# Layer 0 of a CIN tower: from one fp32 product to three fp32r products per sum

## The reference

```python
e = jnp.stack([tbl_f[ids[:, f]] for f in range(39)], axis=1)      # [1024, 39, 16]
x0 = xk = e
for W in (f0, f1, f2):                  # [39*39, 128], [128*39, 128], [128*39, 128]
    z = einsum('bfd,bgd->bfgd', x0, xk).reshape(b, f * g, d)
    xk = einsum('bpd,pm->bmd', z, W)    # [b, 128, 16]
    outs.append(xk)
z = concatenate(outs, axis=1).sum(-1)   # [1024, 384]
h = concatenate([z, dense_ctx], axis=1) # [1024, 400]
h = relu(h @ W_top1 + b_top1); h = relu(h @ W_top2 + b_top2)
y = h @ W_top3                          # [1024, 1]
```

## Time and profile before

| | us |
|---|---|
| median of 3 runs | 1385.07 |
| profiled execution | 1389.53 |
| its span, first to last instruction | 1387.5 |
| TensorE busy | 1304.8 |
| VectorE busy | 1125.3 |
| ScalarE busy | 907.9 |
| GpSimd busy | 703.4 |

### The profile page before, as it was taken

How to read it: one execution, slowest core, us unless ns; L and a number is a source line. 1 busy time by engine, 2 the same in 40 slices (tenths; PEclk the granted TensorE clock), 3 DMA queues, 4 the chain that set the end, 5 groups by cost and what they waited for, 6 DMA issues and landing times.

```text
span 1387.5 us, 20075 instructions
## 1 busy us (share of the span) xinstructions
PE 1304.8 (94%) x5856; PEld 987.6 (71%) x5856; DVE 1125.3 (81%) x2794; ACT 907.9 (65%) x3233; POOL 703.4 (51%) x697
## 2 busy tenths in 40 slices
PE   1189999999999999999999999999999999999998
PEld 0156776777777777777777777777777777777787
DVE  0178988888888888888888888888888888888875
ACT  1046776766767676677767667676766777676664
POOL 6687556654545556454566545455564532333200
PEclk9999999999999999999999999999999999999999
DMA  4081021100311012110211003110121102110000
GB/s 104 17 236 44 21 70 50 49 27 4 94 31 43 27 35 70 50 30 13 70 50 49 28 3 94 31 42 27 35 71 49 30 12 68 47 47 27 1 1 1
DMA packets 52266, 62.47 MB, mean 45 GB/s; under 512 B 13619, under 2 KB 25637, under 8 KB 52156
## 3 DMA queue, kind: packets, MB, share of 16 engines
q1 hardware_dynamic: 34554, 54.64, 12.8%
q0 software_dynamic: 10128, 2.98, 2.1%
q10 hardware_dynamic: 7473, 3.56, 1.0%
HBM read 10.02 MB, written 0.00 MB: 7 GB/s over the span
## 4 chain that ended last, share of the span: by engine, by line
PE 88%; DVE 4%; ACT 3%; issue 3%; ACTq 2%; DMA 1%; SPq 0%; DVEq 0%
PE Y L749 20%; PE Y L751 19%; PE Y L750 19%; PE C L697 14%; PE C L711 5%; PE S L705 5%; ACT Y L473 2%; ACTq L237 2%; PE C L729 1%; PE S L671 1%; DMA G<-in_L_rec_f_dram 1%; DVE sum_b L616 1%; DVE sum_a L616 1%; PE C L719 1%; ACT h L480 1%
## 5 line engine op out<-in xcount | busy, mean ns | idle before, releaser
L473 ACT ACTIVATE Y<-Y,x_col 128x128 f32<-128x128 f32 x2944 | 801.4, 358 | 391.8 <-PE Y L751 351.0
L749 PE MATMUL Y<-f_high,cur_high 128*128 128x512 f32 (+1 forms) x1280 | 627.0, 490 | 8.7 <-DVE part L629 3.5
L751 PE MATMUL Y<-f_high,cur_low 128*128 128x512 f32 (+1 forms) x1280 | 497.6, 389 | 0.0
L750 PE MATMUL Y<-f_low,cur_high 128*128 128x512 f32 (+1 forms) x1280 | 496.9, 388 | 0.0
L373 POOL TENSOR_TENSOR pairs<-shifted,base 117x512 f32<-117x512 f32 x186 | 240.6, 1295 | 462.8 <-PE C L697 460.9
L335 POOL DMA_INDIRECT rows<-in_tbl_dram,ids_sb x312 | 304.9, 977 | 82.4 <-issue 64.9
L749 PEld LDWEIGHTS Y<-f_high,cur_high 128*128 128x128 f32 x1280 | 240.6, 188 | 121.4 <-issue 47.5
L750 PEld LDWEIGHTS Y<-f_low,cur_high 128*128 128x128 f32 x1280 | 241.6, 189 | 92.0 <-issue 52.2
L751 PEld LDWEIGHTS Y<-f_high,cur_low 128*128 128x128 f32 x1280 | 240.0, 188 | 50.8
L616 DVE SCALAR_TENSOR_TENSOR sum_b<-Y,x_col,sum_b 128x128 f32<-128x128 f32 x768 | 262.1, 341 | 0.0
L697 PE MATMUL C<-pairs,f_sum 117*128 117x512 f32 (+1 forms) x448 | 230.0, 596 | 6.4 <-DVE pairs L579 6.2
(11 more groups left out here) (80 smaller groups left out, 643.6 us busy)
## 6 DMA issues: line engine op xcount, KB each, us to landing
shifted<-x_seq SPq DMA_DIRECT2D x157, 234.0 KB
base<-x_seq SPq DMA_DIRECT2D x95, 78.0 KB
rows<-in_tbl_dram,ids_sb POOLq DMA_INDIRECT x312
shifted<-x_seq SPq DMA_DIRECT2D x31, 156.0 KB
G<-in_L_rec_f_dram ACTq DMA_DIRECT2D x3, 832.0 KB, 6.0
w_sb<-in_W_top_dram SPq DMA_DIRECT2D x1, 768.0 KB
w_sb<-in_W_top_dram SPq DMA_DIRECT2D x1, 512.0 KB
shifted<-x_seq ACTq DMA_DIRECT2D x2, 234.0 KB
```

The costliest lines, as they stand in the source:

```text
L473: ins = act.activation(where[:, i * M:(i + 1) * M], where[:, i * M:(i + 1) * M], ACT.Copy, scale=x_col[:, t // JT % QG, t % JT, f:f + 1])
L749: pe.matmul(where, ch, wh, start=True, stop=False)
L750: pe.matmul(where, ch, wl, start=False, stop=False)
L751: pe.matmul(where, cl, wh, start=False, stop=True).then_inc(y_filled, 1)
```

## The change

Layer 0's sum becomes three fp32r products: high weights with high products, low weights with high products, high weights with low products.

- ScalarE rounds each piece of products to fp32r (`round_pair`, a Copy of up to 117x512 from SBUF to SBUF) at given slots of its program, behind that slot's scaling.
- GpSimd subtracts the rounded from the exact piece (`pair_low`). In group 0 VectorE does it (`first_pair_low`).
- The exact products have a ring of two buffers, high and low parts rings of three. So `pair` waits for the low part of two pieces before, `round_pair` for the sum of three pieces before, and the sum for its low part.
- The weights are split once at the start: VectorE adds the mirrored halves into `f0_direct`, ScalarE rounds them, VectorE subtracts.
- The sums move to slots 9, 12, 15, 18, 21, 25, 28; in groups with an MLP they stay at 12 to 30. The roundings stand behind slots 38 (piece 0, a group ahead), 1, 5, 10, 14, 18, 20; in groups with an MLP behind 4, 8, 14, 15, 19, 21. For a group with q = 0 (and group 1) piece 0 isn't rounded ahead: its pieces 0, 1, 2 are rounded behind slots 1, 4, 8.
- GpSimd makes the products 0 and 1 a group ahead, at tile 3. Its steps for tiles 0 to 2 hold four operations each, with a gather behind each as far as there are any.
- 18 gathers of batch tile 1 instead of 16 are made before group 0, three of them behind the first spreading; later gathers are shared 2, 2, 2, 3 over the four tiles of a group.
- `sum_a`, `sum_b` and `part` lose their second buffer; `h1`, `h2`, `y` and `y_col` lie in `rows_seq`. ScalarE issues the output's DMAs, one for each batch tile, instead of SP's two.

```diff
 RING = 3
+PAIR_RING = 2
-AT_SUM = [12 + 3 * k for k in range(K0)]
+AT_SUM = [9, 12, 15, 18, 21, 25, 28]
+AT_SUM_MLP = [12, 15, 18, 21, 24, 27, 30]
+AT_ROUND = [None, 1, 5, 10, 14, 18, 20]
+AT_ROUND_MLP = [1, 4, 8, 14, 15, 19, 21]
+ROUND_AHEAD = 38
-EARLY = 16
-FIRST_EARLY = 4
+EARLY = 18
+FIRST_EARLY, LAST_EARLY = 4, 3
+GATHER_SHARE = (2, 2, 2, 3)
+def first_round_ahead(g):
+    return g % QG != 0 and g >= 2
+def rounds_in_group(g):
+    places = AT_ROUND_MLP if mlp_in_group(g) is not None else AT_ROUND
+    if first_round_ahead(g + 1):
+        return [None] + places[1:]
+    return AT_ROUND_MLP[:3] + places[3:]
...
             def pair(g, k):
-                pool.wait_ge(cur0_summed, z - RING + 1)
...
+                if g == 1 and k < PAIR_RING:
+                    pool.wait_ge(first_low, K0)
+                else:
+                    pool.wait_ge(low_ready, z - K0 - PAIR_RING + 1)
+            def pair_low(g, k):
+                pool.wait_ge(pairs_rounded, z + 1)
+                pool.tensor_tensor(pairs_low[0:r, z % RING, :], pairs[0:r, z % PAIR_RING, :],
+                                   pairs_high[0:r, z % RING, :].bitcast(F32), ALU.subtract).then_inc(low_ready, 1)
+            LOW_STEPS = ((("low", 0), ("pair", 2), ("low", 1), ("pair", 3)),
+                         (("low", 2), ("pair", 4), ("low", 3), ("pair", 5)),
+                         (("low", 4), ("pair", 6), ("low", 5), ("low", 6)),
+                         ())
...
-            gather(1, range(FIRST_EARLY, EARLY))
+            gather(1, range(FIRST_EARLY, EARLY - LAST_EARLY))
+            for k in (0, 1):
+                pair(1, k)
...
             spread(0)
+            gather(1, range(EARLY - LAST_EARLY, EARLY))
...
+                    if j == JT - 1 and g + 2 < NG and first_round_ahead(g + 2):
+                        for k in (0, 1):
+                            pair(g + 2, k)
...
                     if j == JT - 1 and g + 1 < NG:
                         spread(g + 1)
+                    if j == JT - 1 and g + 2 < NG and not first_round_ahead(g + 2):
+                        for k in (0, 1):
+                            pair(g + 2, k)
...
+            def round_pair(g, k):
+                if g:
+                    act.wait_ge(pairs_ready, z - K0 + 1)
+                else:
+                    act.wait_ge(first_pairs, k + 1)
+                if z >= RING:
+                    act.wait_ge(cur0_summed, z - RING + 1)
+                act.activation(pairs_high[0:r, z % RING, :], pairs[0:r, z % PAIR_RING, :], ACT.Copy)\
+                   .then_inc(pairs_rounded, 1)
...
+            def first_pair_low(k):
+                dve.wait_ge(pairs_rounded, k + 1)
+                dve.tensor_tensor(pairs_low[0:r, k % RING, :], pairs[0:r, k % PAIR_RING, :],
+                                  pairs_high[0:r, k % RING, :].bitcast(F32), ALU.subtract).then_inc(first_low, 1)
...
-                    pe.wait_ge(pairs_ready, z - K0 + 1)
+                    pe.wait_ge(low_ready, z - K0 + 1)
...
-                pe.matmul(C[:], f0_sum[0:r, k, :], pairs[0:r, z % RING, :],
-                          start=k == 0, stop=k == K0 - 1).then_inc(cur0_summed, 1)
+                high, low = pairs_high[0:r, z % RING, :], pairs_low[0:r, z % RING, :]
+                pe.matmul(C[:], f0_sum[0:r, k, :], high, start=k == 0, stop=False)
+                pe.matmul(C[:], f0_low[0:r, k, :], high, start=False, stop=False)
+                pe.matmul(C[:], f0_sum[0:r, k, :], low, start=False, stop=k == K0 - 1).then_inc(cur0_summed, 1)
```

More of the change, by code:

```diff
@@ L126, in gathers_in_tile @@
     step, u = divmod(t + AHEAD, TPB)
-    u, tiles = u - 2, TPB - 2
-    if step + 1 >= BT or u < 0:
-        return None
-    return step + 1, range(NF * u // tiles, NF * (u + 1) // tiles)
+    if step + 1 >= BT or u < 2:
+        return None
+    share = [GATHER_SHARE[(v - AHEAD) % JT] for v in range(2, TPB)]
+    done, all_ = sum(share[:u - 2]), sum(share)
+    return step + 1, range(NF * done // all_, NF * (done + share[u - 2]) // all_)
 def build(nc, dense, ids, tables, w1, b1, w2, b2, w3, f0, f1, f2, out):
@@ L312, in _ @@
                                  allow_slow_non_contiguous=True).then_inc(mlp_in, 16)
[L313 to L318, removed]
+            sp.wait_ge(y_out, 16 * BT)
         @blk.gpsimd
@@ L396, in _ @@
                         pool.wait_ge(rows_taken, len(ROW_PARTS) * (now[0] - 1))
-                    if q == 1 and j >= 2 and bt + 1 < BT:
-                        for part in ((0, 1), (2, 3))[j - 2]:
-                            take_rows(bt + 1, part)
[L400 to L403, removed]
+                    if j == JT - 1 and g + 2 < NG and first_round_ahead(g + 2):
+                        for k in (0, 1):
+                            pair(g + 2, k)
+                    if q == 1 and j == JT - 1 and bt + 1 < BT:
+                        for part in (2, 3):
+                            take_rows(bt + 1, part)
+                    steps = LOW_STEPS[j] if g + 1 < NG else ()
+                    for i in range(max(len(steps), len(fs))):
+                        if i < len(steps):
+                            kind, k = steps[i]
+                            (pair if kind == "pair" else pair_low)(g + 1, k)
                         if i < len(fs):
@@ L407, in _ @@
                         spread(g + 1)
+                    if j == JT - 1 and g + 2 < NG and not first_round_ahead(g + 2):
+                        for k in (0, 1):
+                            pair(g + 2, k)
+                    if q == 1 and j == JT - 2 and bt + 1 < BT:
+                        for part in (0, 1):
+                            take_rows(bt + 1, part)
         @blk.scalar
@@ L602, in fuse @@
                 for i, f in enumerate(CH_F[c]):
-                    acc = (sum_a if c < 4 else part, sum_b)[(i + starts) % 2][:, t % 2, :]
+                    acc = (sum_a[:] if c < 4 else part[:], sum_b[:])[(i + starts) % 2]
                     src = bank(t, c)[:, i * M:(i + 1) * M]
```

101 lines of the change are left out of this document (72 added, 29 removed).

## The result

The changed kernel takes 1397.39 us (median of 4 runs, 1395.9 to 1398.19) against 1385.17; the ratio is 1.0083, 95% interval 1.0071 to 1.0095. Forecast was 1377.5, range 1361 to 1395. The profiled execution took 1396.6 us, its span is 1394.9, granted clock 0.996. Against the earlier trace rows, its page: engines, chain, sums.

What follows compares the result with a forecast made beforehand. The prediction took TensorE, 94% busy, to bound the kernel, with little slack in the ring with ScalarE and VectorE. A start cost of 11.1 us less 18.6 us gained in groups gave -7.5 us, so 1377.5 us, range 1361 to 1395.

Steps and rivals of the forecast that it cites:

- The price of one sum: On TensorE, one layer 0 sum falls from 0.86 to 0.70 us as three fp32r products 0.23 us apart.
- The start: Before the first chunk, VectorE's added subtractions and waits for roundings put the first chunk at 86.8 us, +3.4.
- Group 0: First group: GpSimd's queue has the low part of product 6 at 120.7 us, TensorE wants it at about 113.
- q = 0: Groups with the MLP, 41.8 us: sums keep their places, 1.1 less 0.2 for a GpSimd wait, gain 0.9.
- q = 1: Steady group, 39.5 us: ScalarE's block of 15 scalings, lengthened by two roundings, then VectorE; 38.9, gain 0.6.
- They push slot 18 back by 0.6: 39.5, gain 1.0: Groups with q = 2, 40.5 us: sixteen transposes delay slot 18 by 0.6, giving 39.5 us.
- I get 40.4, a loss of 0.2: Groups with q = 3, 40.2 us: late GpSimd products, product 6 ready at 23.5 us, hold ScalarE's rounding and scalings.
- Groups 1 to 4: Groups without layer 2, where TensorE waits for VectorE: some 1.2 us gained in three, nothing in the fourth, 3.7.
- The sum: Whole kernel: +11.1 us at the start and -18.6 in the groups make -7.5 us, median 1377.5.
- Rival 2: GpSimd and in-order ScalarE form a loop at slot 20's rounding, 0.3 to 0.8 us per group: +2 to +16; chance 0.27.
- Rival 1: TensorE bounds everywhere: -34 + 11 = -23 us, 1362 us; chance 0.15.
- The rule weighed: GpSimd and two-SBUF-input VectorE instructions lock a shared port: steady state untouched, start 10 us more by the slow row.

Runs made afterwards that it cites:

- e1: Changed kernel without the gathers for batch tiles 1 to 7, which use the rows of the first: 1376.39 us against 1385.74 for the kernel before.
- e2: Changed kernel without GpSimd's low parts from group 1 on; TensorE multiplies the rounded products once more instead: 1377.76 us, ratio 0.9949 to the kernel before.
- e6: Changed kernel with all gathers kept but moved to other tiles: 1388.07 us, ratio 1.0023 to the kernel before.
- e4: Changed kernel with the last rounding of a group behind slot 21 instead of 20, outside MLP groups: 1394.43 us, ratio 1.0067 to the kernel before.
- e3: Changed kernel without ScalarE's roundings from group 1 on; the low part is a product minus itself, used three times: 1370.33 us, ratio 0.9886.
- e9: Changed kernel with only the sums moved to slots 12 to 30 in every group, roundings left in place: 1389.4 us against 1395.6 for the kernel before.
- e5: Changed kernel with sums and roundings at the places of the MLP groups everywhere: 1375.78 us against 1385.83 for the kernel before.
- e12: Changed kernel with sums at 12 to 30, first gathers moved, MLP rounding places except in q = 1: 1369.97 us against 1384.77 for the kernel before.
- e14: Changed kernel, unchanged, profiled a second time on the same chip as the kernel before: 1396.61 us.
- e13: Kernel before, unchanged, profiled a second time on the same chip as the changed kernel: 1384.71 us.

## Why the prediction was wrong

- **The price of one sum: right.** 0.70 us, three records 0.23 apart.
- **The start: right** (+3.6 against +3.4). By its own terms the working gives 84.4 and not 84.0 for the last low part, and so +3.7. The first profile of before had a start 5.7 us longer than its second, so the two first spans differ by 7.4 where the medians differ by 12.2.
- **Group 0: right in mechanism, short by 1.5.** e1, e2 and e6 show that GpSimd's queue made it. The low part of product 6 was ready 34.2 us behind the first chunk, where 33.9 and 0.7 for slower gathers were forecast; but its sum came 1.2 later, since TensorE had waited for earlier low parts and then run at half clock, 1.2 GHz, and that was not in the sum. Group 1 started at 129.1, not near 132, because the forecast stood on the late start of the first profile.
- **q = 0: right**, by its own steps. **q = 1: the size right, the chain wrong.** e4 took away the second rounding of the block and nothing changed. Slot 28 decides, and seven sums stand before it where six stood. Group 21, 1.0 us longer than the others, was not foreseen.
- **"They push slot 18 back by 0.6: 39.5, gain 1.0": this step failed.** It gave q = 2 the chain of q = 1 and forgot what else the same roundings delay: the reading of bank S. Six groups, 6 us. Of the 1.0 in each, e4 brings back 0.5 and e3, without any rounding, 0.7. The other 0.3 stays open; e9 gets 0.7 back with the sums' places alone.
- **"I get 40.4, a loss of 0.2" (q = 3): mis-sized.** Mechanism right (e1, e2, e6: 39.8), the size is 1.4. Product 6 was ready 24.1 us into the group, forecast 23.5, and ScalarE waited 0.96 us for it. The low part of product 5 came late by 0.61 and not by 1.2, but TensorE also waited 0.79 us at slot 21, for which the sum had nothing. Five groups, 6 us; in the sixth, group 27, no gathers are left, and it gained 0.7.
- **Groups 1 to 4: failed, 4.4 us.** Group 3 is a q = 3 without layer 2: I gave it no change, it lost 2.0, with three waits for low parts of 0.54 to 0.77 us. Group 2 gained nothing, like q = 2. Groups 1 and 4 gained 0.6 each, not 1.2.
- **The sum:** the span was to change by -7.5 us and changed by +12.1. Of the 19.6 between them q = 2 has 6.3, q = 3 5.3, groups 1 to 4 4.4, group 0 1.5, group 21 1.0, the end 0.5 and the start 0.2.
- **Rival 2** had the loop, ScalarE in order behind GpSimd, but not its place: it acts in q = 3 and group 0, not in all. That the time lies in its range (+2 to +16) is in good part luck, since q = 2 and groups 2, 1 and 4 brought as much from other causes. **Rival 1** is refuted.
- **The rule weighed:** VectorE's adds kept 342 ns with GpSimd at 70%. In the start, gathers beside VectorE's low parts took 1.1 us, not 0.95, in sum about 1 us: far less than the 10 that the slow row would have made. It did lie on the path: VectorE's last low part ended at 79.2, and GpSimd came to its first product only at 80.5.

Open: what makes GpSimd pause before the 270th gather; the 0.3 us of q = 2 that no rounding explains; and what ended the start of the first profile of before so late.

## What to carry to other kernels

When work moves from the bound engine to engines that execute in order, price the places and not the sums: each added instruction delays all behind it, also reads that only free a bank. Put an instruction that may wait on a third engine where its own engine idles: for q = 3 the later roundings were worth 1.4 us a group here, but only once the sums stood late (e9 to e5); with early sums the move from slot 20 to 21 was worth nothing there (e4). Where two waits stand one behind the other, taking away one shows nothing. A saving on the bound engine is lost if its work is moved away from the stretch where the others need the time: the same change cost 12 us or gained 15 us (e12) by the places of sums, roundings and first gathers alone.

## What the runs showed of the hardware

Two waits of TensorE of 1.9 us in group 0 were each followed by a stretch at 1.2 GHz (granted clock 0.58 and 0.57 in windows of 4 us), in which products of 512 columns stood 0.43 us apart instead of 0.23; a wait of 1.54 us in e14 was not. Group 0 of the kernel before took 38.9 us with such a stretch (e13) and 37.9 without. GpSimd's subtraction with an fp32r result took as long as its multiplication in fp32, 1.29 us. GpSimd stood still for 2.5 to 4.0 us before its 270th gather in twelve of fourteen traces, and nothing in them shows for what.
